# Attention scores of both heads as plain fp32 products in row halves, and all key tiles of the late queries turned by VectorE and DMAs

## The chip, the cores and the metric

One NeuronCore of a Trainium2 chip runs the whole kernel. The metric is device time in microseconds of one execution.

## The reference

A layer of post-norm attention followed by a routed feed-forward layer, all in fp32, on 8 sequences of 1024 tokens with 256 channels:

```python
latent_kv = x @ w_kv_down                 # rank 128
kv = latent_kv @ w_kv_up
k, v = (kv[..., :HD], kv[..., HD:])       # 16 heads of 64
q = (x @ w_q).reshape(Bx, Tx, N_HEAD, HEAD_SIZE)
att = jnp.einsum('bqhd,bkhd->bhqk', q, k) * scale
att = jnp.where(causal, att, -jnp.inf)
att = jax.nn.softmax(att, axis=-1)
y = jnp.einsum('bhqk,bkhd->bqhd', att, v)
x = layernorm(x + y.reshape(Bx, Tx, HD) @ w_out)
x = layernorm(x + experts(x))             # 8 experts, top tokens of each, gelu
```

The change is in the attention up to y; the output projection, the routing and the experts stay as they are.

## The kernel before, in words

`attention_stage` goes through 64 head pairs n (8 sequences, 8 pairs of heads each; "batch" is a sequence). Each engine has its own program, written out by hand, and semaphores tie them. A pair has 16 steps s, one for each query tile q = 0 to 7 of 128 queries and each head h. Query tile q has (q + 1) * 128 keys, since the mask is causal. For a step:

- TensorE computes the scores (`scores`, L443 and L444) into `s_ps`. Queries and keys are split in high and low fp32r parts. The tile `q_hl` of a head has the high part in the head's own 64 rows and the low part in the other 64; `k_hh` has the high keys in both halves, `k_lz` the low keys and zeros. So a first product gives high*high + low*high and a second high*low.
- VectorE adds the mask and takes the negated maximum (`maximum`, L734); ScalarE takes the exponential and its sum (`exp`, L623) into `prob`, one of four buffers; VectorE takes the reciprocal (`invert`, L739); GpSimd scales the tile (`norm`, L281).
- The probabilities are turned, so that keys lie in partitions. TensorE does it with an identity (`turn`, L453) for all tiles of q < 4 and for key tiles 0 to 3 of the late queries q >= 4; ScalarE and VectorE copy the result out of PSUM (`tri`, `prob_t`). Key tiles 4 to 7 of the late queries are turned in 32x32 squares by VectorE (`turn_squares`, L761) into `squares`; a DMA writes these to `s_d` in HBM (`write_squares`, L341) and four DMAs read them back, each to 32 partitions (`read_squares`, L349), into `late_t`.
- TensorE multiplies values and turned probabilities (`pv`, L476), 64 columns a head, so the two heads stand in the two column halves of the array: group 0 the early queries, group 1 the late ones. VectorE copies `o_ps` out (`copy_y`, L768), a DMA stores it.

Beside that, each pair needs projections of the pairs to come: queries (12 fp32r products of 512 columns, L519 to L521), keys (6, L532 to L534), values (8 fp32 products, L551). ScalarE takes the high part (`high`, L631), VectorE the low part (`low`, L747, L750), and ten DMAs of 256 KB (`place_queries`, `place_keys`) bring the parts to the rows where the scores want them. When a batch ends, the next x and its latents are split too. The order is set by tables, for instance

```python
SCORES_AT = [[4], [5], [6], [7], []] + [[s + 3] for s in range(5, 13)] + [[16], [17, 18], [19]]
INVERSES_AT = [[2], [3], [], [6], [7], []] + [[s + 2] for s in range(6, 16)]
Q_AT, K_AT, V_AT = (12, 15), (2, 5), (8, 10)
```

so the scores of a pair begin in the last steps of the one before, and the reading of `late_t` (`pv` of group 1, key tiles 4 to 7) stands in step 7 of the next pair. All DMAs here are issued by SP, one after the other (`turn` of the sync program).

Of the kernel before, what the change touches and what calls it, by code (L numbers as in the profile page):

```python
# [8 lines left out]
F32 = mybir.dt.float32  # L9
F32R = mybir.dt.float32r  # L10
# [29 lines left out]
class Bridge:  # L40
# [3 lines left out]
    def __init__(self, sb, sem, L):  # L44
# [3 lines left out]
        self.q_hl = [L.w1_hi[:, h * T:(h + 1) * T] for h in range(2)]  # L48
        self.k_hh = [L.w1_lo[:, h * T:(h + 1) * T] for h in range(2)]
# [4 lines left out]
        self.yt = [w[:].bitcast(F32).rearrange("p (m c) -> p m c", c=HALF) for w in (*self.q_hl, *self.k_hh)]  # L54
# [5 lines left out]
def attention_stage(nc, x_t, w_down, w_q, w_k, w_v, y_d, s_d, w_out, R):  # L60

    NPAIRS = B * NPAIR
    TRI = 2 * (4 + 3 + 2 + 1) * P

    Q = 32

    Q_AT, K_AT, V_AT = (12, 15), (2, 5), (8, 10)
    with ExitStack() as ctx:
# [4 lines left out]

# [3 lines left out]
        wd_hi = sb("wd_hi", [P, KC, RANK], F32R)  # L81
        wd_lo = sb("wd_lo", [P, KC, RANK], F32R)

        lat_hi = sb("b_lat_hi", [P, T], F32R)
        lat_lo = sb("b_lat_lo", [P, T], F32R)

        wqk = [sb(f"wqk{u}", [P, KC + 1, P]) for u in range(2)]
        wqk_hi = [sb(f"wqk_hi{u}", [P, KC + 1, P], F32R) for u in range(2)]
        wqk_lo = [sb(f"wqk_lo{u}", [P, KC + 1, P], F32R) for u in range(2)]
        wv = [sb(f"wv{u}", [P, P]) for u in range(2)]  # L90

        q_hl = [R.q_hl, [sb(f"q_hl1{h}", [P, T], F32R) for h in range(2)]]

        k_hh = [R.k_hh, [sb(f"k_hh1{h}", [P, T], F32R) for h in range(2)]]


        k_lz = [[sb(f"k_lz{u}{h}", [P, T], F32R) for h in range(2)] for u in range(2)]


        q_high, q_low, k_high, k_low = (sb(n, [P, T], F32R) for n in ("q_high", "q_low", "k_high", "k_low"))  # L100
        v = [sb(f"v{u}", [P, QT, P]) for u in range(2)]
        prob = [sb(f"prob{i}", [P, T]) for i in range(4)]

        wd = prob[3][:, 0:KC * RANK].rearrange("p (k r) -> p k r", r=RANK)

        tri = sb("tri", [P, TRI])
        prob_t = sb("prob_t1", [P, 2, 4, HALF])
        late_t = sb("late_t", [P, 4, 4, 8 * Q])  # L110

        squares = [sb(f"squares{i}", [P, (24 + 8 * i) * 4 * Q // 4]) for i in range(2)]
        neg_max = sb("neg_max", [P, 4])
        total = sb("total", [P, 4])
        inv = sb("inv", [P, 4])
# [7 lines left out]
        const_ready, x_in = sem("const_ready"), sem("b_x_in")  # L123


        x_then_q, wd_then_k = sem("x_then_q"), sem("wd_then_k")
# [5 lines left out]
        late_in = sem("late_in")  # L132
        squares_out = [sem(f"squares_out{i}") for i in range(2)]
        copied = [sem("copied_a"), sem("copied_d")]
# [5 lines left out]
        proj_done, high_done, low_done, v_copied, q_placed, k_placed = (  # L140
            sem(n) for n in ("proj_done", "high_done", "low_done", "v_copied", "q_placed", "k_placed"))
        block = ctx.enter_context(nc.Block())

        def step(s):

            return s // 8, 4 * (s // 8) + s % 8 // 2, s % 2

        def count(s):

            return min(4, step(s)[1] + 1)  # L150
# [11 lines left out]
        def square_part(w, h):  # L162

            return squares[(w - 1) % 2][:, 0:8 * w * Q].rearrange("p (j h k c) -> p j h k c", j=4, h=2, c=Q)[:, :, h, :, :]

        def late_row(h, k):

            at = k * 32 * Q + h * (k + 1) * Q + k * Q
            return bass.AP(tensor=late_t[:].tensor, offset=at, ap=[[128 * Q, P], [32 * Q + h * Q, 4 - k], [8 * Q, 4], [1, Q]])

        def turned_to(s):

            g, q, h = step(s)
            return tri_column(h, q) if g == 0 else prob_t[:, h, :, (q - 4) * P:(q - 3) * P]

        def score_at(s):

            return s_ps[s % 2], (s // 2 % 2 * HALF if s < 8 else 0)
# [1952 lines left out]
```

## Time and profile before

| | |
|---|---|
| median of 3 runs | 3088.05 us (3086.75 to 3089.26) |
| the profiled execution | 3095.27 us, its span 3093.4 us |
| TensorE, VectorE, ScalarE, GpSimd busy | 97%, 67%, 62%, 50% |
| mean granted TensorE clock | 0.989 |
| bytes moved by DMAs | 544.63 MB, mean 176 GB/s |
| HBM read, written | 213.16 MB, 159.47 MB |

Busy shares are of the span, in which the first 2040 us or so are the attention stage. A wait is idle time of an engine before an instruction, put down to what released it. A matmul's duration in a row includes its way through the array, so two that follow each other overlap: how much one costs is the distance of their starts. An fp32 product is two instructions on TensorE, an fp32r product one.

### The profile page before, as it was taken

The numbers are of one execution on the slowest core, as the hardware profiler recorded it, in microseconds if no ns is written. First come the engines' busy times: TensorE is split into PE (matmuls) and PEld (weight loads), VectorE is DVE, ScalarE is ACT, GpSimd is POOL, SyncE is SP. The second block draws the span as 40 slices with busy tenths as digits, with TensorE's granted clock in tenths as the row PEclk, the third lists the DMA queues.
The fourth block names the chain that finished last, engine by engine and source line by source line (L and its number), as shares of the span: only waits on it lengthen the run. The fifth ranks groups of instructions, "written<-read, shape, count | busy, mean of one in ns | idle before, by whom it ended". The sixth has DMA issues, their size and how long they took to land. (4 is left out here: it accounts for less than half of the span.)

```text
span 3093.4 us, 62741 instructions
## 1 busy us (share of the span) xinstructions
PE 2991.5 (97%) x19244; PEld 2394.3 (77%) x19244; DVE 2079.3 (67%) x5938; ACT 1910.0 (62%) x4173; POOL 1539.8 (50%) x1623
## 2 busy tenths in 40 slices
PE   8999999999999999999999999979989999999996
PEld 6776767776767776676767677679989999899996
DVE  6776777777767777676776777634968865545446
ACT  6676767777767777676767777635534444444443
POOL 4443444444444443444444344336767776666665
PEclk9999999999999999999999999989989999999998
DMA  7787877786777777777777787677734444434425
GB/s 182 202 205 186 205 207 190 202 212 188 201 205 189 196 202 192 197 198 208 186 203 209 192 208 203 167 242 267 242 112 122 115 103 105 106 78 91 110 50 163
DMA packets 397585, 544.63 MB, mean 176 GB/s; under 512 B 79528, under 2 KB 295976, under 8 KB 397248
## 3 DMA queue, kind: packets, MB, share of 16 engines
q1 hardware_dynamic: 355200, 490.05, 57.9%
q0 software_dynamic: 25152, 33.75, 6.6%
q10 hardware_dynamic: 16896, 16.78, 1.5%
q8 instruction: 157, 2.57, 0.3%
q14 instruction: 180, 1.47, 0.1%
HBM read 213.16 MB, written 159.47 MB: 120 GB/s over the span
## 5 line engine op out<-in xcount | busy, mean ns | idle before, releaser
L281 POOL TENSOR_SCALAR prob<-prob,inv 128x128 f32<-128x128 f32 (+7 forms) x1024 | 766.7, 752 | 1137.0 <-DVE inv L739 1136.6
L734 DVE CUSTOM_DVE_ANT_0 s_ps<-s_ps,mask 128x128 f32<-128x128 f32 (+7 forms) x1024 | 774.2, 756 | 445.1 <-PE s_ps L444 438.6
L623 ACT ACTIVATE prob<-s_ps,neg_max 128x128 f32<-128x128 f32 (+7 forms) x1024 | 760.3, 743 | 218.3 <-DVE neg_max L734 210.3
L453 PE MATMUL t_ps<-ident,prob 128*128 128x128 f32 x3328 | 527.3, 275 | 24.8 <-POOL prob L281 18.4
L453 PEld LDWEIGHTS t_ps<-ident,prob 128*128 128x128 f32 x3328 | 394.1, 141 | 75.9 <-POOL prob L281 23.4
L716 ACT ACTIVATE prob_t<-t_ps 128x512 f32<-128x512 f32 x512 | 305.8, 597 | 208.3 <-PE t_ps L453 208.2
L1791 PE MATMUL e_y<-w_hi,hid_hi 128*128 128x256 f32 (+1 forms) x1088 | 312.6, 287 | 0.0
L1793 PE MATMUL e_y<-w_hi,hid_lo 128*128 128x256 f32 (+1 forms) x1088 | 308.8, 284 | 0.0
L1792 PE MATMUL e_y<-w_lo,hid_hi 128*128 128x256 f32 (+1 forms) x1088 | 308.7, 284 | 0.0
L1652 POOL DMA_INDIRECT acc_d<-yg,idx_all x128 | 211.3, 1651 | 189.8 <-ACT yg L1865 160.9
L443 PE MATMUL s_ps<-w_lo,w_hi 128*128 128x512 f32 (+3 forms) x768 | 291.9, 382 | 7.4 <-ACT prob L623 7.4
L443 PE MATMUL s_ps<-k_hh,q_hl 128*128 128x512 f32 (+3 forms) x768 | 293.8, 385 | 4.6 <-ACT prob L623 4.5
L761 DVE STREAM_TRANSPOSE squares<-prob 128x128 f32<-128x128 f32 (+3 forms) x512 | 255.4, 499 | 54.2 <-DMA s_d<-squares 52.5
L1899 ACT ACTIVATE raw<-e_h,b1s 128x384 f32<-128x384 f32 (+3 forms) x336 | 193.8, 586 | 133.8 <-PE e_h L1774 128.3
L444 PE MATMUL s_ps<-k_lz,q_hl 128*128 128x512 f32 (+3 forms) x768 | 257.8, 348 | 0.0
L444 PE MATMUL s_ps<-k_lz,w_hi 128*128 128x512 f32 (+3 forms) x768 | 256.1, 346 | 0.0
L476 PE MATMUL o_ps<-prob_t,v 128*64 128x512 f32 x1024 | 237.1, 605 | 13.4 <-DMA late_t<-s_d 9.8
L1772 PE MATMUL e_h<-tok_hi,w_hi 128*128 128x384 f32 (+3 forms) x672 | 230.2, 343 | 1.7 <-DVE tok_lo L1937 1.2
L1773 PE MATMUL e_h<-tok_lo,w_hi 128*128 128x384 f32 (+3 forms) x672 | 230.1, 342 | 0.0
L1774 PE MATMUL e_h<-tok_hi,w_lo 128*128 128x384 f32 (+3 forms) x672 | 229.7, 342 | 0.0
L2033 DVE CAST hid_hi<-raw 128x384 fp32r<-128x384 f32 (+3 forms) x336 | 129.6, 386 | 121.9 <-ACT raw L1899 115.4
L1865 ACT ACTIVATE yg<-yb,gate_all 128x256 f32<-128x256 f32 x128 | 59.1, 502 | 239.6 <-DVE yb L2068 239.5
(261 smaller groups left out, 6732.0 us busy)
## 6 DMA issues: line engine op xcount, KB each, us to landing
k_hh<-k_high SPq DMA_DIRECT2D x128, 256.0 KB, 4.5
s_d<-squares SPq DMA_DIRECT2D x64, 512.0 KB, 3.0
y_d<-c_res SPq DMA_DIRECT2D x128, 256.0 KB, 4.0
late_t<-s_d SPq DMA_DIRECT2D x256, 128.0 KB, 3.3
k_lz<-k_low SPq DMA_DIRECT2D x126, 256.0 KB, 5.4
w_lo<-k_high SPq DMA_DIRECT2D x124, 256.0 KB, 4.5
c_yt<-y_d SPq DMA_DIRECT2D x60, 512.0 KB, 7.3
s_d<-squares SPq DMA_DIRECT2D x64, 384.0 KB, 2.6
```

The lines of the kernel that those rows point to most:

```text
L281: pool.tensor_scalar(pr, pr, inv[:, s % 4:s % 4 + 1], 1.0, ALU.mult, ALU.mult).then_inc(norm_done, 1)
L443: pe.matmul(out, q_hl[u][h][:, cols], k_hh[u][h][:, w], start=True, stop=False)
L444: mm = pe.matmul(out, q_hl[u][h][:, cols], k_lz[u][h][:, w], start=False, stop=True)
L453: mm = pe.transpose(t_ps[s % 2][:, to * P:(to + 1) * P], prob[s % 4][:, j * P:(j + 1) * P], ident[:])
L476: mm = pe.matmul(o_ps[64 * h:64 * h + 64, off:HALF], v[u][:, k, 64 * h:64 * h + 64], keys, start=(k == 0), stop=(k == 4 * g + 3), skip_gro ...
L623: act.activation(prob[s % 4][:, 0:(q + 1) * P], score_part(s), ACT.Exp, scale=-1.0, bias=neg_max[:, s % 4:s % 4 + 1], accum_out=total[:, s ...
L716: act.activation(turned_to(s), t_ps[s % 2][:, 0:count(s) * P].rearrange("p (j c) -> p j c", c=P), ACT.Copy).then_inc(copied[s % 2], 1)
L734: dve.tensor_tensor_reduce(part, part, mask[:, T - (q + 1) * P:T], 1.0, -MASKED, ALU.add, ALU.min, neg_max[:, s % 4:s % 4 + 1]).then_inc(m ...
L761: dve.transpose(square_part(w, h), prob[s % 4][:, HALF:HALF + w * P].rearrange("p (k j c) -> p j k c", j=4, c=Q)).then_inc(squared, 1)
L1791: pe.matmul(out, hid_hi[:, m, cols], w2_hi[u][:, w], start=(m == 0), stop=False)
L1792: pe.matmul(out, hid_hi[:, m, cols], w2_lo[u][:, w], start=False, stop=False)
L1793: mm = pe.matmul(out, hid_lo[:, m, cols], w2_hi[u][:, w], start=False, stop=(m == HC - 1))
```

## The change

Both heads' scores are fp32 products: head h uses rows 64h to 64h + 63 of the projected queries and keys where they are, one product for each head and 512 keys, in the two row halves of the array. The high and low parts of queries and keys, `low`, the zeros of `k_lz` and the ten placements a pair are gone. `turn` on TensorE and its copies are left for q < 4 alone; for q >= 4 all q + 1 key tiles go by `turn_squares`, `s_d` and `late_t`. `late_t` is double, `prob` has eight buffers in place of four, PSUM has three score units of two banks (one of them holds the turned early tiles), and `neg_max`, `total`, `inv` have eight columns. A reciprocal takes two heads at once. The output copies `copy_y` go from VectorE to ScalarE, the low parts of x and the latents of later batches from VectorE to GpSimd. The tables are replaced by eight slots a pair, one for each query tile; loops of SP are written out. The split weights and latents live in the space that `q_hl` and `k_hh` had.

The core of the diff (`-` before, `+` after):

```diff
-        s_ps = [pb(f"s_ps{i}", [P, T]) for i in range(2)]
-        t_ps = [pb(f"t_ps{i}", [P, HALF]) for i in range(2)]
+        s_ps = [pb(f"s_ps{i}", [P, T]) for i in range(3)]
...
+        def unit(n, role):
+            return s_ps[(role - n) % 3]
+
+        def score_part(n, s):
+            q, h = s // 2, s % 2
+            width = (q + 1) * P
+            if q < 4:
+                return unit(n, q % 2)[:, h * HALF:h * HALF + width]
+            return unit(n, (s - 8) % 3)[:, 0:width]
+
+        def turned_part(n, q, h):
+            return unit(n, 2)[:, h * HALF:h * HALF + (q + 1) * P]
...
-                    pe.matmul(out, q_hl[u][h][:, cols], k_hh[u][h][:, w], start=True, stop=False)
-                    mm = pe.matmul(out, q_hl[u][h][:, cols], k_lz[u][h][:, w], start=False, stop=True)
-                mm.then_inc(scores_done, 1)
...
+            def scores(n, q):
+                cols = slice(q * P, (q + 1) * P)
+                width = (q + 1) * P
+                for c in range(1 + q // 4):
+                    w = slice(c * HALF, min((c + 1) * HALF, width))
+                    for h in range(2):
+                        rows = slice(64 * h, 64 * h + 64)
+                        mm = pe.matmul(score_part(n, 2 * q + h)[:, w], q_of[n % 2][rows, cols], k_of[n % 2][rows, w],
+                                       start=True, stop=True)
+                        if c == q // 4:
+                            mm.then_inc(scores_done, 1)
...
+                elif q == 5:
+                    pe.wait_ge(copied, 4 * n + 4)
+                    pe.wait_ge(copied_last, n + 1)
+                    pe.wait_ge(exp_done, 16 * n + 9)
+                elif q > 5:
+                    pe.wait_ge(exp_done, 16 * n + 2 * q - 1)
...
+            def slot(n, q):
...
+                scores_free(n, q)
+                scores(n, q)
+                if q == 0:
+                    project_v(n, 0)
+                    if n >= 2:
+                        pv(n - 2, 1, [7])
+                if q == 1:
+                    project_v(n, 1)
+                    if n:
+                        pv(n - 1, 0, range(4))
+                    turn(n, 0)
+                if q == 2:
+                    if last_of_batch(n):
+                        project_l(n // NPAIR + 1, 0)
+                    turn(n, 1)
+                if q == 3:
+                    if last_of_batch(n):
+                        project_l(n // NPAIR + 1, 1)
+                    if after:
+                        project_q(n + 1, 0)
+                    turn(n, 2)
+                if q == 4:
+                    if after:
+                        project_k(n + 1, 0)
+                    turn(n, 3)
+                    if after:
+                        project_q(n + 1, 1)
+                if q == 5 and n:
+                    pv(n - 1, 1, [0, 1, 2])
+                if q == 6:
+                    if n:
+                        pv(n - 1, 1, [3, 4])
+                    if after:
+                        project_k(n + 1, 1)
+                if q == 7 and n:
+                    pv(n - 1, 1, [5, 6])
...
+            def turn_squares(n, q):
+                t = q + 1
+                for h in range(2):
+                    dve.wait_ge(norm_done, 16 * n + 2 * q + h + 1)
+                    if h == 0:
+                        dve.wait_ge(squares_out[q % 2], 16 * (2 * n + (q - 4) // 2))
+                    dve.transpose(square_all(q).rearrange("p (j h k c) -> p j h k c", j=4, h=2, c=Q)[:, :, h, :, :],
+                                  prob[(2 * q + h) % PB][:, 0:t * P].rearrange("p (k j c) -> p j k c", j=4, c=Q)
+                                  ).then_inc(squared, 1)
```

Slot q of a pair on VectorE has the two maxima of tile q; `turn_squares` of tiles 4 and 5 stand in slots 6 and 7, those of tiles 6 and 7 in slots 0 and 2 of the next pair. On ScalarE slot q has the two exponentials of tile q, on GpSimd the two norms.

Three places in the order. VectorE where one pair ends and the next begins; maxima are the rows with `s_ps,neg_max`, their width is the number of keys. Before:

```order
L734 ISA s_ps,neg_max<-s_ps,mask 128x1024 [waits scores_done]
L734 ISA neg_max 128x1
L739 RECIPROCAL inv<-total 128x1 [waits exp_done]
L761 STREAM_TRANSPOSE squares<-prob 128x4x96 [waits squares_out0,pv_done1,norm_done]
L734 ISA s_ps,neg_max<-s_ps,mask 128x128 [waits scores_done]
L734 ISA neg_max 128x1
L739 RECIPROCAL inv<-total 128x1 [waits exp_done]
L761 STREAM_TRANSPOSE squares<-prob 128x4x96 [waits squares_out0,pv_done1,norm_done]
```

Now:

```order
L631 ISA s_ps,neg_max<-s_ps,mask 128x1024 [waits scores_done]
L631 ISA neg_max 128x1
L637 RECIPROCAL inv<-total 128x2 [waits exp_done]
L645 STREAM_TRANSPOSE squares<-prob 128x4x192 [waits squares_out1,norm_done]
L645 STREAM_TRANSPOSE squares<-prob 128x4x192 [waits norm_done]
L631 ISA s_ps,neg_max<-s_ps,mask 128x128 [waits scores_done]
L631 ISA neg_max 128x1
L631 ISA s_ps,neg_max<-s_ps,mask 128x128 [waits scores_done]
L631 ISA neg_max 128x1
L645 STREAM_TRANSPOSE squares<-prob 128x4x224 [waits squares_out0,norm_done]
L645 STREAM_TRANSPOSE squares<-prob 128x4x224 [waits norm_done]
```

Turns of one head's squares, one between two maxima, have become two wide ones in a row, after both maxima of a tile. On TensorE, slots 5 to 7 of the new order (`tok` holds the queries and keys of every second pair):

```order
L323 MATMUL s_ps<-tok 128x256 x2
L368 MATMUL o_ps<-late_t,v 64x512 [waits y_copied,v_copied,late_in0]
L368 MATMUL o_ps<-late_t,v 64x512 x5
L323 MATMUL s_ps<-tok 128x512 [waits exp_done]
L323 MATMUL s_ps<-tok 128x512
L323 MATMUL s_ps<-tok 128x384 x2
L368 MATMUL o_ps<-late_t,v 64x512 x4
```

The products that read `late_t` now stand between the scores of tiles 5 and 6; the first of them waits for all 16 reads of the pair before. On SP, in each pair:

```order
L255 DMA s_d<-squares 128x2048 [waits squared]
L265 DMA late_t<-s_d 32x4x448 [waits squares_out0]
L265 DMA late_t<-s_d 32x4x448 x3
L250 DMA y_d<-c_res 128x512 [waits y_copied]
L265 DMA late_t<-s_d 32x4x512 [waits squares_out1]
L265 DMA late_t<-s_d 32x4x512 x3
L242 DMA wqk<-w_q 128x2x128 [waits proj_done]
```

The last write has 2048 columns where the largest had 1024, and the placements that stood behind the reads are gone.

## Rows read from the trace of the kernel before

**Rows 1.** the page, busy time, share of the span and instructions of each engine

```profile
PE 2991.5 (97%) x19244; PEld 2394.3 (77%) x19244; DVE 2079.3 (67%) x5938; ACT 1910.0 (62%) x4173; POOL 1539.8 (50%) x1623
```

**Rows 2.** the line of the masked maximum: count, min/median/max ns, first and last start

```profile
L734 DVE CUSTOM_DVE_ANT_0 s_ps<-s_ps,mask x1024: 266/775/1233, 23.9 to 2007.0; 128x128 f32<-128x128 f32 x22, 128x512 f32<-128x512 f32 x22, 128x896 f32<-128x896 f32 x22, 128x256 f32<-128x256 f32 x21
```

**Rows 3.** busy time by window: TensorE, weight load, VectorE, ScalarE, GpSimd, clock, DMA share, GB/s

```profile
600.00:900.00 300.00, 296.81 (x1778) 213.04 (x1779) 216.10 (x651) 214.86 (x508) 126.46 (x167) 1.00 0.76 201
```

**Rows 4.** timeline of TensorE in one pair: start us, us, engine, line, operation

```profile
641.40 3.65 PE L476 MATMUL o_ps<-prob_t,v 128*64 128x512 f32 x16
...
644.99 0.50 PE L443 MATMUL s_ps<-w_lo,w_hi 128*128 128x512 f32 x1
...
646.47 0.40 PE L443 MATMUL s_ps<-w_lo,w_hi 128*128 128x512 f32 x1
646.70 0.40 PE L444 MATMUL s_ps<-k_lz,w_hi 128*128 128x512 f32 x1
...
650.48 0.62 PE L453 MATMUL t_ps<-ident,prob 128*128 128x128 f32 x4
...
650.91 0.50 PE L443 MATMUL s_ps<-w_lo,w_hi 128*128 128x512 f32 x1
```

**Rows 5.** VectorE by form: busy us, mean ns, idle before

```profile
L734 DVE CUSTOM_DVE_ANT_0 s_ps<-s_ps,mask 128x1024 f32<-128x1024 f32 x128 | 156.0, 1219 | 65.1 <-PE s_ps L444 64.9 <-issue 0.2
...
L734 DVE CUSTOM_DVE_ANT_0 s_ps<-s_ps,mask 128x128 f32<-128x128 f32 x128 | 37.5, 294 | 47.7 <-PE s_ps L444 43.2
...
L761 DVE STREAM_TRANSPOSE squares<-prob 128x512 f32<-128x512 f32 x128 | 89.7, 701 | 6.9 <-DMA s_d<-squares 6.5 <-POOL prob L281 0.3
...
L761 DVE STREAM_TRANSPOSE squares<-prob 128x128 f32<-128x128 f32 x128 | 37.5, 293 | 0.0
```

**Rows 6.** timeline of VectorE, same pair

```profile
647.28 0.70 DVE L734 CUSTOM_DVE_ANT_0 s_ps<-s_ps,mask 128x512 f32<-128x512 f32 x1 [0.62 <-PE s_ps L444]
...
657.85 1.10 DVE L734 CUSTOM_DVE_ANT_0 s_ps<-s_ps,mask 128x896 f32<-128x896 f32 x1 [0.31 <-PE s_ps L444]
...
669.84 0.69 DVE L761 STREAM_TRANSPOSE squares<-prob 128x512 f32<-128x512 f32 x1
670.45 0.40 DVE L734 CUSTOM_DVE_ANT_0 s_ps<-s_ps,mask 128x256 f32<-128x256 f32 x1
```

**Rows 7.** DMA issues of the whole run: count, KB each, median us to landing

```profile
k_hh<-k_high SPq DMA_DIRECT2D x128, 256.0 KB, 4.5
...
s_d<-squares SPq DMA_DIRECT2D x64, 512.0 KB, 3.0
...
s_d<-squares SPq DMA_DIRECT2D x64, 384.0 KB, 2.6
...
late_t<-s_d SPq DMA_DIRECT2D x256, 128.0 KB, 3.3
```

**Rows 8.** timeline of ScalarE, same pair

```profile
659.04 1.01 ACT L623 ACTIVATE prob<-s_ps,neg_max 128x896 f32<-128x896 f32 x1 [0.31 <-DVE neg_max L734]
...
659.95 0.19 ACT L623 ACTIVATION_READ_ACCUMULATOR prob<-s_ps,neg_max 128x1 f32 x1
```

**Rows 9.** GpSimd by form

```profile
L281 POOL TENSOR_SCALAR prob<-prob,inv 128x1024 f32<-128x1024 f32 x128 | 143.2, 1118 | 109.1 <-DVE inv L739 109.1
...
L281 POOL TENSOR_SCALAR prob<-prob,inv 128x128 f32<-128x128 f32 x128 | 47.6, 372 | 150.6 <-DVE inv L739 150.5
```

**Rows 10.** timeline of the DMA queue, same pair

```profile
643.95 1.89 SPq L349 DMA_DIRECT2D late_t<-s_d  x4
```

**Rows 11.** timeline of TensorE around a stretch at half clock

```profile
918.38 0.90 PE L453 MATMUL t_ps<-ident,prob 128*128 128x128 f32 x4 [1.74 <-POOL prob L281]
...
919.50 0.63 PE L520 MATMUL j_ps<-b_xt_lo,wqk_hi 128*128 128x512 f32 x1
919.92 0.63 PE L521 MATMUL j_ps<-b_xt_hi,wqk_lo 128*128 128x512 f32 x1
```

**Rows 12.** busy time by window, the stretch at half clock

```profile
918.70:922.00 3.30, 3.30 (x12) 2.73 (x10) 2.29 (x8) 1.29 (x6) 0.59 (x2) 0.50 0.81 265
```

More of the change, by code:

```diff
@@ L195, in attention_stage @@
-        LATE_EXPS_AT = {0: [3]}
-        def over_pairs(eng, first, slots):
-            first()
-            for n in range(NPAIRS):
-                after = min(2, NPAIRS - 1 - n)
-                for g in range(2):
-                    slots(n, n % NPAIR, g, after)
-        X_SPLIT = [(NPAIR - 2, s) for s in (0, 2, 4, 6)]
-        L_AT = (11, 14)
-        W_SPLIT = 4
-        def x_piece(b, i):
-            if isinstance(b, int) and b == 0:
-                return i % 2, halves(i // 2)
-            return i // 2, halves(i % 2)
@@ new lines, in last_of_batch, with over_pairs, x_piece, x_pieces @@
+        def last_of_batch(n):
+            return n % NPAIR == NPAIR - 1 and n < NPAIRS - 1
+        def over_pairs(slot):
+            for n in range(NPAIRS):
+                for q in range(8):
+                    slot(n, q)
+        X_SPLIT = [(NPAIR - 2, 6), (NPAIR - 2, 7), (NPAIR - 1, 0), (NPAIR - 1, 1)]
+        def x_piece(i):
+            return i % 2, halves(i // 2)
+        def x_pieces(n, q):
+            at = (n % NPAIR, q)
+            return [X_SPLIT.index(at)] if at in X_SPLIT and n // NPAIR < B - 1 else []
@@ new lines, in turn @@
+            def turn(n, q):
+                if q:
+                    pe.wait_ge(copied, 4 * n + q)
+                elif n:
+                    pe.wait_ge(exp_done, 16 * n)
+                for h in range(2):
+                    pe.wait_ge(norm_done, 16 * n + 2 * q + h + 1)
+                    for j in range(q + 1):
+                        to = q - j if h else j
+                        mm = pe.transpose(turned_part(n, q, h)[:, to * P:(to + 1) * P],
+                                          prob[(2 * q + h) % PB][:, j * P:(j + 1) * P], ident[:])
+                    mm.then_inc(turned, 1)
@@ L616, in _ @@
+            over_pairs(slot)
+            pv(NPAIRS - 2, 1, [7])
+            pv(NPAIRS - 1, 0, range(4))
+            pv(NPAIRS - 1, 1, range(8))
         @block.scalar
@@ new lines, in exp, with keep @@
+                i = s % PB
+                act.activation(prob[i][:, 0:(q + 1) * P], score_part(n, s), ACT.Exp, scale=-1.0,
+                               bias=neg_max[:, i:i + 1], accum_out=total[:, i:i + 1]).then_inc(exp_done, 1)
+            def keep(n, i):
+                act.wait_ge(proj_done, proj(n, i))
+                to = (q_of, k_of)[i % 2][n % 2]
+                act.activation(to[:, halves(i // 2)], proj_bank(n, i), ACT.Copy,
+                               scale=1.0 if i % 2 else -SCALE).then_inc(high_done, 1)
```

793 lines of the change are left out of this document (326 added, 467 removed).

## The prediction

> **What bounds the kernel now.** I read the page first: TensorE is busy for 97% of the span, the next engine for 67% [rows 1]. Then the line of the masked maximum: 1024 of them, 16 a head pair, the first at 23.9 us and the last at 2007.0 us [rows 2], so a pair takes 1983/64 = 31.0 us and the change touches some 1984 us of the span. In a steady stretch, 600 to 900 us, TensorE is busy for 296.8 of 300 us at full clock, and VectorE, ScalarE and GpSimd for 216, 215 and 126 [rows 3]. The timeline of TensorE shows one product behind the other: the two passes of a 512-column score product start 0.23 us apart (646.47 and 646.70), four turns 0.43 us (650.48 to 650.91), the next product starts in the same moment [rows 4]. So a pair costs 31.0 us because TensorE has about that much to do.
>
> **TensorE's part.** Scores. A head's 36 key tiles of 128 columns took two passes of 0.23 us for 512 columns, 0.9 ns a column: 4.1 us, narrow ones a little more, 8.6 us for two heads, plus some 0.1 us at each of 16 entries after turns (a first product of 0.50 against 0.40 us in [rows 4]): 10.2. They become plain fp32 products with 64 rows, one head in each row half. No row shows row halves. The nearest shows fp32 in the two column halves: 16 instructions, two for each product, took 641.40 to 644.99 = 3.59 us for 4 key tiles of 512 columns and both heads [rows 4], so 0.43 us a pass for both heads together, 1.68 ns a column for a finished pair. I take that: 36 x 128 x 1.68 = 7.7 us and 8 entries of 0.1: 8.5. That is the lower end. The upper is the halves one after the other, 15.5 + 0.8. Turns: 32 of 52 go (four key tiles, two heads, four late query tiles), 32 x 0.108 = 3.5 us. Projections and values keep their products. TensorE: 31.0 - 1.7 - 3.5 = 25.8 us a pair. This alone would be a gain of 330 us, so the question is what is late next.
>
> The Trainium skill, TensorEngine Tiling, section Key Properties, says that a change of tiling mode drains TensorE. The run of 16 column-half products agrees weakly: 3.59 us against 8 x 0.43 = 3.44, so 0.15 for entry and exit. If a drain cost the pipeline's 0.35 us instead, the 16 changes of mode would add 4 us to TensorE and 0.75 to the loop below, giving some 3385.
>
> **The other engines.** VectorE loses the low halves (4 x 0.6), two output copies (1.2), the small copies and half the reciprocals, and turns 52 blocks in place of 20. A turn costs 0.293 us at 128 columns and 0.701 at 512 [rows 5], 0.136 for each further block: widths 640 to 1024 give 0.84, 0.97, 1.11, 1.25, less the 0.08 that consecutive operations overlap (669.84 to 670.45 is 0.61 for one of 0.69 [rows 6]). 7.7 us a pair against 3.4; all of VectorE about 20 us. ScalarE loses eight late copies and takes two output copies and four turned copies: 18 to 19. GpSimd 14. None of them fills 31 us, and none needs a price beyond these rows unless it stands in a chain.
>
> DMAs. Gone are ten placements of 256 KB a pair [rows 7]. Squares grow from 1.3 to 3.4 MB, written and read again: 7.7 MB a pair in place of 6.2. They were busy for 0.76 of the steady stretch [rows 3], so 0.95 of 31 us at the same efficiency, 29 us; the old placements had packets that were the slow ones, so likely less. Not the bound, but the round trip is longer.
>
> **The loop that I expect to set the time.** The new order on VectorE puts both turns of a query tile between one score group and the next, and SP carries them out and back. I follow what must follow what, from the scores of query tile 6 to the same scores one pair later (maximum 128 wide 0.294, 1024 wide 1.219 [rows 5], so 0.132 a block, 0.08 overlapped):
> - scores of tile 6: 896 x 1.68 + 0.1 = 1.6; to VectorE 0.35 (646.70 + 0.23 of columns to 647.28 in [rows 4, 6]);
> - maximum of tile 6 until its exponential starts 1.19 (657.85 to 659.04), that until its sum is read 1.12 [rows 6, 8]. The score unit of tile 7 is free only then;
> - scores of tile 7: 1.8 + 0.35; its two maxima 2.28; reciprocal and both turns of tile 5: 0.08 + 1.78;
> - next pair's maxima of tile 0: 0.43; both turns of tile 6: 2.06; maxima of tile 1: 0.65; reciprocals of tiles 7 and 0: 0.16, to GpSimd 0.25;
> - GpSimd: norms of tile 7 two x 1.12, of tile 0 two x 0.37 + 0.1 [rows 9]; the turn of tile 0 on TensorE 0.11; scores of tile 2: 0.74 + 0.35; maxima of tile 2: 0.96;
> - both turns of tile 7: 2.34 + 0.15; their 1 MB write. 512 KB land in 3.0 us, 384 KB in 2.6 [rows 7], 0.35 for 128 KB more: 4.5. The read, four DMAs of 256 KB issued over 2 us (the four of 128 KB took 1.89 [rows 10]); one of 128 KB lands 3.3 after its issue, and 1 MB more is on the way: 5.5;
> - the late product of values and tiles 0 to 2, 2.66 (three of 0.86, 0.1), stands ahead of the scores of tile 6.
>
> Sum: 1.95 + 1.19 + 1.12 + 2.15 + 2.28 + 1.86 + 0.43 + 2.06 + 0.65 + 0.41 + 2.24 + 0.84 + 0.11 + 1.09 + 0.96 + 2.49 + 4.5 + 5.5 + 2.66 = **34.5 us a pair**. TensorE idles about 9 of them, in four places: second values projection behind a ScalarE copy (slot 1), turn 0, turn 2, and the late product. Each batch edge adds the two latent projections and splits, some 3 us in 8 pairs: 34.9. That is 3.9 x 64 = +250 us. The profiled execution took 3095.3 us, 7 above the median: 3095 + 250 - 7 = 3338, and I say **3335**. Start and end change by a few us either way (no placements at the start; a longer trip at the end). The trip's price is my softest: at 0.85 and 1.15 of it the loop is 33.0 and 36.0, 3240 and 3430.
>
> **Rivals.**
> 1. The trip hides. If write and read take under 8 us in place of 10, a shorter loop decides: from the end of the turns of tile 7 (21.7) on, maximum of tile 6 of columns 0.62, reciprocal 0.33, norms of tile 2 1.27, turn 2 0.42, scores 4 1.17, projections and turn 3 3.1, scores 5 1.38, late product 2.66: 32.6, with edges 33.0: +128, 3216. For: landings there are seen beside 2.6 MB of placements that go.
> 2. The clock falls. It was granted at half from 918.7 to 922.0 us [rows 12], right after TensorE had waited 1.74 us for GpSimd with only narrow scores and turns around: the next 512-column products start 0.43 apart (919.50, 919.92), not 0.23 [rows 11]. The new order has waits of 1 to 3 us in each pair. Such a stretch of 3.3 us in each pair costs up to 1.7 us, most where TensorE has slack: at most +110, 3445. [...]
> 3. The row halves don't run together: the change doesn't do what it says. The loop's three score groups grow by 1.5, 1.7 and 0.6: 38.3, edges 38.7: +493, 3580. Against it: the column halves do.
> 4. **Faster**: TensorE still decides. Everything that I put in a chain would have to be ready earlier, so that less than 5.2 us of waits stand beside 25.8 us of work. Without waits 25.8 + 0.4 = 26.2: -307, 2780; with half of my waits 30.7, 3070. It decides from the point where the loop is below 31.0, 3.5 us under my sum; the trip at half its price and norms of tile 7 out of the way of tile 0 would do. For it speaks that each engine has a third of the time free; against it that the order is fixed and both engines take turns in it.
>
> **Numbers.** Forecast 0.51, rival 1 0.14, rival 2 0.14, rival 3 0.07, rival 4 0.14 (0.02 of it within the bound). The range takes the forecast with the trip's bounds, and rivals 1 and 2: 3180 to 3460, 0.79. A measurement of this kernel can tell 0.2%, 6 us, from no change. Faster 0.13 (rival 4 but for a sliver), same 0.02, slower 0.85.
>
> **What would show it.** Pair distance (last less first maximum, over 64) near 34.9. Scores: both heads' products start together, 0.43 us a 512-column pass; else rival 3. Waits of TensorE: late products for late_t, turns for prob by GpSimd, in sum 6 us a pair or more; if the DMA's share is nil, rival 1; if all are under 3, rival 4. s_d writes of 1 MB landing in 4 to 5 us. Granted clock under 0.95 in the attention stage: rival 2. If pair distance is right but waits stand elsewhere, the sum was luck.

## The result and the profile after

The changed kernel takes **3895.54 us** (median of 4 runs, 3890.03 to 3903.06), the kernel before beside it 3088.66 us (4 runs, 3086.75 to 3089.58). The ratio is 1.261, 95% interval 1.260 to 1.263: slower by 807 us. Forecast were 3335 us and a range up to 3460. The direction was right, the size was not. Two of the seven runs of the kernel before that stand beside e11 and e12 below were slow ones at a lower clock (3290 and 4837 us), and all ratios are of the fast runs.

The profiled execution took 3892.69 us, its span 3890.8, with a mean granted clock of 0.892 (before 0.989). TensorE is busy for 80% of the span, VectorE 51%, ScalarE 45%, GpSimd 40%: against [rows 1] no engine is busy throughout any more. The line of the masked maximum, with durations in ns and the first and last start in us:

```profile
engine op xcount: duration ns min/median/max, first and last start us, forms
L631 DVE CUSTOM_DVE_ANT_0 s_ps<-s_ps,mask x1024: 265/766/1267, 18.0 to 2795.6; 128x128 f32<-128x128 f32 x22, 128x512 f32<-128x512 f32 x22, 128x896 f32<-128x896 f32 x22, 128x256 f32<-128x256 f32 x21
```

(2795.6 - 18.0) / 64 = **43.4 us a pair**, against 31.0 before [rows 2] and 34.9 forecast. 12.4 us in 64 pairs are 794 of the 807 us, so nearly all of it is in the attention stage. The stretches of the steady part (busy us of each engine, then granted clock, share of the DMA engines, GB/s); the three short ones lie in one pair, and a share a little over 1 is to be read as full:

```profile
core 0: us, PE busy (x) PEld busy (x) DVE busy (x) ACT busy (x) POOL busy (x), PEclk, DMA share, GB/s
800.00:1200.00 400.00, 298.06 (x1395) 142.33 (x1391) 189.58 (x453) 183.28 (x455) 124.82 (x165) 0.86 0.66 181
938.00:943.00 5.00, 5.00 (x31) 3.27 (x27) 2.31 (x5) 3.13 (x7) 0.30 (x1) 1.00 0.97 224
943.00:948.00 5.00, 0.03 (x2) 0.00 (x0) 1.96 (x5) 1.93 (x4) 1.58 (x2) 0.71 1.06 245
948.00:950.60 2.60, 0.00 (x0) 0.00 (x0) 0.00 (x0) 0.00 (x0) 0.00 (x0) 0.50 0.78 130
```

TensorE's waits from 800 to 1200 us, which are 9.2 pairs (us in total, times, longest):

```profile
PE o_ps L368 <- DMA late_t<-s_d: 63.6, 9, 8.0
PE j_ps L429 <- ACT v L509: 20.6, 9, 2.3
PE s_ps L351 <- POOL prob L202: 16.2, 10, 1.8
```

Seven us a pair go to `late_t` alone. Around the longest wait the timeline of TensorE reads (start, us, and in brackets the idle time before):

```profile
936.00 1.02 PE L351 MATMUL s_ps<-ident,prob 128*128 128x128 f32 x6 [1.66 <-POOL prob L202]
936.95 1.35 PE L323 MATMUL s_ps<-tok 64*128 64x512 f32 x8
938.23 0.50 PE L414 MATMUL j_ps<-w_hi 128*128 128x512 f32 x1
...
941.47 1.56 PE L323 MATMUL s_ps<-tok 64*128 64x512 f32 x8
950.66 5.08 PE L368 MATMUL o_ps<-late_t,v 128*64 128x512 f32 x12 [7.63 <-DMA late_t<-s_d]
955.66 1.77 PE L323 MATMUL s_ps<-tok 64*128 64x512 f32 x8
```

and that of SP's queue:

```profile
934.49 0.34 SPq L255 DMA_DIRECT2D s_d<-squares  x1
934.94 2.91 SPq L265 DMA_DIRECT2D late_t<-s_d  x4
937.96 0.43 SPq L250 DMA_DIRECT2D y_d<-c_res  x1
939.71 1.73 SPq L265 DMA_DIRECT2D late_t<-s_d  x4
```

The turns of tile 7 are done at 934.5, and their write is issued. Its four reads are issued at 939.7, the product that needs them starts at 950.66. The trip from the last write to the late product is 16.2 us here, and the forecast had 10.0. The trace also has the landings: the last read of tile 6 at 944.4, the y store at 944.8, the four reads of tile 7 from 946.1 to 950.6. So of the 10.9 us after the write, the first 5.1 went by while the queue was still busy with what stood ahead. Then the late product of key tiles 0 to 2 takes 5.08 us, not 2.66: the clock fell to 0.50 during the wait. DMA issues and the queue's share from 800 to 1200 us (KB each, median us from issue to landing):

```profile
q1 hardware_dynamic: 34754, 72.05, 65.5%
...
s_d<-squares SPq DMA_DIRECT2D x10, 1024.0 KB, 5.1
late_t<-s_d SPq DMA_DIRECT2D x36, 256.0 KB, 7.5
late_t<-s_d SPq DMA_DIRECT2D x40, 224.0 KB, 6.9
```

The scores did what the change says: in the timeline above the eight instructions of tile 4 take 1.28 us to the start of the next product (936.95 to 938.23), and one pair earlier those of tile 6 take 1.70 (912.11 to 913.81):

```profile
912.11 1.77 PE L323 MATMUL s_ps<-k,q 64*128 64x512 f32 x8
913.81 1.94 PE L368 MATMUL o_ps<-late_t,v 128*64 128x512 f32 x8
```

The forecast had 1.2 and 1.6. The two row halves run side by side. By the forecast's 1.68 ns a column, 0.2 us of each group, up to the start of the next product, are not columns, where the sum had 0.1; and the scores of tile 5 start 0.32 us after a product (941.15, 941.47) whose like lie 0.23 apart. The reading that gave 3385 us had 0.35 at each change of mode, more than either.

### The profile page after: what moved, and what is told of

The parts are those of the page before. It is cut to its first block and busy times, and to the rows that moved or that the text cites. A ratio compares the mean times of both kernels' runs of the same rounds, so it can differ in the third digit from the quotient of the medians.

```text
span 3890.8 us, 53342 instructions
## 1 busy us (share of the span) xinstructions
PE 3104.0 (80%) x17196; PEld 1979.4 (51%) x17196; DVE 1968.5 (51%) x4808; ACT 1766.1 (45%) x3981; POOL 1570.1 (40%) x1661
## 5 line engine op out<-in xcount | busy, mean ns | idle before, releaser
L368 PE MATMUL o_ps<-late_t,v 128*64 128x512 f32 (+3 forms) x2048 | 557.9, 679 | 469.8 <-DMA late_t<-s_d 469.8
L368 PEld LDWEIGHTS o_ps<-late_t,v 128*64 128x64 f32 x2048 | 153.2, 167 | 801.2 <-DMA late_t<-s_d 495.4
L645 DVE STREAM_TRANSPOSE squares<-prob 128x640 f32<-128x640 f32 (+3 forms) x512 | 500.9, 1016 | 2.0 <-DMA s_d<-squares 2.0
L323 PE MATMUL s_ps<-k,q 64*128 64x512 f32 (+3 forms) x1536 | 322.7, 525 | 3.4 <-ACT prob L498 3.4
L323 PE MATMUL s_ps<-tok 64*128 64x512 f32 (+3 forms) x1536 | 321.4, 523 | 3.6 <-ACT prob L498 2.6
L351 PE MATMUL s_ps<-ident,prob 128*128 128x128 f32 x1280 | 212.5, 287 | 106.1 <-POOL prob L202 105.5
L429 PE MATMUL j_ps<-wv,b_lat 128*128 128x128 f32 x1024 | 165.0, 309 | 144.5 <-ACT v L509 144.1
L351 PEld LDWEIGHTS s_ps<-ident,prob 128*128 128x128 f32 x1280 | 141.1, 142 | 209.0 <-issue 142.9
L368 PE MATMUL o_ps<-tri,v 128*64 128x512 f32 (+3 forms) x1024 | 240.5, 633 | 3.1 <-ACT c_res L523 3.1
L429 PEld LDWEIGHTS j_ps<-wv,b_lat 128*128 128x128 f32 x1024 | 137.3, 208 | 178.3 <-ACT v L509 170.2
```

The costliest lines, as they stand in the source:

```text
L323: mm = pe.matmul(score_part(n, 2 * q + h)[:, w], q_of[n % 2][rows, cols], k_of[n % 2][rows, w], start=True, stop=True)
L351: mm = pe.transpose(turned_part(n, q, h)[:, to * P:(to + 1) * P], prob[(2 * q + h) % PB][:, j * P:(j + 1) * P], ident[:])
L368: mm = pe.matmul(o_ps[64 * h:64 * h + 64, off:HALF], v[n % 2][:, k, 64 * h:64 * h + 64], keys, start=(k == 0), stop=(k == 4 * g + 3), skip ...
L645: dve.transpose(square_all(q).rearrange("p (j h k c) -> p j h k c", j=4, h=2, c=Q)[:, :, h, :, :], prob[(2 * q + h) % PB][:, 0:t * P].rear ...
```

## The experiments

Each kernel is the changed one with the edit shown. Its time stands beside runs of the kernel before on the same chip (medians 3088 to 3094 us). "A pair" is the last less the first maximum of the profiled run, over 64, as above.

| run | edit | us | ratio, interval | us a pair | clock, 800 to 1200 us |
|---|---|---|---|---|---|
| before | | 3088 | | 31.0 | |
| changed | | 3895.5 | 1.261 [1.260, 1.263] | 43.4 | 0.86 |
| e1 | no reads | 3297.6 | 1.068 [1.065, 1.071] | 34.4 | 0.96 |
| e2 | reads from two queues | 3834.0 | 1.241 [1.238, 1.245] | 42.5 | 0.86 |
| e3 | filler in the wait | 3772.2 | 1.221 [1.218, 1.225] | 41.5 | 0.96 |
| e4 | late product later | 3580.1 | 1.159 [1.154, 1.165] | 38.4 | 0.92 |
| e5 | spread reads, VectorE pays | 3809.3 | 1.234 [1.230, 1.237] | 42.1 | 0.87 |
| e6 | e5 and e4 | 3730.8 | 1.208 [1.202, 1.215] | 40.8 | 0.88 |
| e7 | spread reads, TensorE pays | 3775.8 | 1.221 [1.209, 1.232] | 41.8 | 0.94 |
| e8 | e7 and e4 | 3750.5 | 1.213 [1.209, 1.216] | 41.2 | 0.92 |
| e9 | spread reads, keys dealt by ScalarE | 3607.9 | 1.167 [1.143, 1.190] | 39.3 | 0.91 |
| e10 | e9 and e4 | 3352.7 | 1.084 [1.079, 1.089] | 35.0 | 0.96 |
| e11 | e10 in a new order | **3015.9** | **0.976 [0.974, 0.978]** | 29.8 | 1.00 |
| e12 | the new order, reads as changed | 3240.1 | 1.048 [1.046, 1.051] | 33.2 | 0.97 |

### Is it the trip? e1, e2

```diff
-                read_squares(n, 4)
+                if n < 2:
+                    read_squares(n, 4)
```

The same for tiles 5 to 7; the waits for `late_t` are on the constant 256. From the third pair on the late product takes what the first two pairs left, so the late queries are not computed. The writes stay.

> The change with the read back of the squares left out from the third pair on (the late products then use old rows of late_t, so the late queries of the output are not the reference's). Writes stay. Theory A (the loop through the trip of the squares sets the pair, and its price was 16 us where 10 were put down): the loop without the trip decides, 32.6 us in steady pairs by the sum of the prediction, 33 with batch edges, and the granted clock of the attention stage rises from 0.86 to over 0.95, since the wait of 7 us goes: some 3220 us, 43.4 to 33 us a pair. Theory B (the clock at half is what costs, the waits are its consequence): the pair falls less, to 38 or more, the clock stays under 0.9. Theory C (TensorE alone would decide without the trip): under 28 us a pair, 2900 us.

Measured: 3297.6 us, 34.4 us a pair. TensorE's waits, for 11.6 pairs:

```profile
PE j_ps L433 <- ACT v L513: 27.5, 12, 2.3
PE s_ps L355 <- POOL prob L202: 20.1, 17, 1.9
```

The time fell with the reads as theory A has it, but 78 us less far than its 3220. So the reads carry 598 of the 807 us; what is left without them, the writes and the order of the engines, 1.4 us a pair above what rival 1 summed, carries the other 209. Of that order one sees two waits: 2.4 us a pair for ScalarE's copy of the values and 1.7 for GpSimd's norms.

```diff
-                for j in range(4):
+                for j in range(2):
...
+                for j in range(2, 4):
+                    act.dma_start(late_t[n % 2][Q * j:Q * j + Q, q - 4, :, 0:2 * t * Q],
```

> The change with two of the four reads of each tile (partitions 64 to 127) issued from ScalarE's queue, so that both halves of the partitions are written at the same time; same bytes, same waits of TensorE. Theory A1 (reads are slow because each read, and so all engines at one time, writes 32 partitions: 228 KB a us in the trace of the change): reads go to 350 to 390 KB a us, the trip from the write of tile 7 to the late product falls from 16 to 11 or 12 us, the pair from 43.4 to 38 or 39, some 3590 us. Theory A2 (the reads are limited by HBM or by the bytes of all DMAs together): no change beyond 1 us a pair, packets of 2048 bytes still take 135 ns at twice the number in flight; ScalarE's issues cost up to 1 us a pair.

Measured: 3834.0, 42.5 us a pair, and a trip of 15.9 us in the pair at 917 us. 256 KB landed in 6.8 us from SP and 8.1 from ScalarE (7.5 before the edit). Theory A1, which had 3590 us, failed: in that pair the reads of tile 7 landed one after the other all the same, those of SP at 928.4 and 929.8, those of ScalarE at 930.7 and 932.5. The issuing is not what makes the reads slow. Whether their partitions are, this edit can't tell.

### How much is the clock? e3

```diff
+                    if after:
+                        pe.wait_ge(high_done, 4 * n + 7)
+                        for _ in range(FILL):
+                            pe.matmul(j_ps[:, 0:256], wd_hi[:, 0, :], wd_hi[:].rearrange("p k r -> p (k r)"),
+                                      start=True, stop=True)
```

56 products a pair, with no use for their result, stand ahead of the late product.

> The change with 56 extra fp32r products of 256 columns (about 6.2 us at full clock) on TensorE between the scores of tile 5 and the late product, into the projection bank, so that TensorE works while it waits for the reads. Nothing else moves. Theory A (half clock after the long wait adds 1.5 to 2.4 us to the late product and about 1 us to the scores and values behind it, all on the loop): late product of tiles 0 to 2 falls from 4.3 to 5.1 us to 2.7, the clock of the stage rises from 0.86 to over 0.95, the pair falls by 2 to 3 us to about 41, some 3740 us. Theory B (the clock's loss lies in slack): clock up, pair unchanged within 0.5 us.

Measured: 3772.2, 41.5 us a pair, **1.9 less**, though work was added. The clock in the window went from 0.86 to 0.96 and the 512-column late products from a mean of 852 ns to

```profile
L369 PE MATMUL o_ps<-late_t,v 128*64 128x512 f32 x180 | 42.6, 602 | 3.9 <-DMA late_t<-s_d 3.9
```

That is just under the 2 to 3 us of theory A. So the fall of the clock behind the long wait costs about 1.9 us a pair, and it costs them on the loop, since the late product is the first thing that the wait holds up.

### How much room does the trip need? e4

```diff
-                if q == 5 and n:
-                    pv(n - 1, 1, [0, 1, 2])
...
-                        pv(n - 1, 1, [3, 4])
+                        pv(n - 1, 1, [0, 1, 2])
```

The rest of the late product follows one tile later too.

> The change with the late products of a pair moved one slot back: tiles 0 to 2 behind the scores of tile 6 (not 5), 3 and 4 in slot 7, 5 to 7 in slot 0. Same work, same bytes. Theory A (the loop goes trip, late product, scores 6, maximum and exponential 6, scores 7): scores 6, its maximum and exponential now run beside the trip, so 1.6 + 0.35 + 2.3 = 4.3 us leave the loop less what the new order adds before copy_y: the pair falls by 3 to 4.5 us to 39 to 40.5, some 3680 us; the wait for late_t falls from 7.5 us to 3 to 4. Theory B (DMA throughput, not the loop, sets the pair): unchanged within 0.5 us, the wait only moves.

Measured: 3580.1, 38.4 us a pair, 5.0 less, more than the 3 to 4.5 expected. The wait for `late_t` is down to 2.5 us a pair (10.4 pairs), and the next ones have come forward:

```profile
PE o_ps L368 <- DMA late_t<-s_d: 25.5, 10, 3.5
PE s_ps L323 <- ACT prob L496: 25.1, 11, 2.3
PE s_ps L351 <- POOL prob L202: 24.3, 26, 2.3
```

### Why are the reads slow? e5 to e10

The four reads of a tile write 32 neighbouring partitions each. In the steady part the queue moved 72.05 MB with 16 engines busy for 65.5% of 400 us: 275 KB per us of full use. In two stretches of the pair shown above in which nearly nothing but these reads ran, the last column shows 226 and 209 GB/s:

```profile
939.70:941.20 1.50, 1.50 (x10) 1.18 (x8) 1.10 (x3) 1.50 (x5) 0.00 (x0) 1.00 0.99 226
945.00:948.00 3.00, 0.00 (x0) 0.00 (x0) 0.18 (x2) 1.20 (x4) 1.04 (x2) 0.51 1.06 209
```

The placements of the kernel before wrote 64 neighbours, and a stretch of them alone (its 648 to 652 us) has 221 GB/s at a share of 0.98. In e5 key 4c + j of a tile, in place of 32j + c, goes to group j, so that a read writes partitions j, j + 4, ..., j + 124.

```diff
-                    sp.dma_start(late_t[n % 2][Q * j:Q * j + Q, q - 4, :, 0:2 * t * Q],
+                    sp.dma_start(late_t[n % 2][j:P:4, q - 4, :, 0:2 * t * Q],
...
-                                  prob[(2 * q + h) % PB][:, 0:t * P].rearrange("p (k j c) -> p j k c", j=4, c=Q)
+                                  prob[(2 * q + h) % PB][:, 0:t * P].rearrange("p (k c j) -> p j k c", j=4, c=Q)
```

> The changed kernel with the keys of a tile dealt out otherwise: key 4c + j, in place of 32j + c, goes into group j, so each of the four reads of a tile writes the 32 partitions j, j + 4, ..., j + 124 of late_t and not 32 neighbours. Same bytes, same packets, same order; VectorE's block turns read their input at a step of four numbers. Theory A (a read is slow because it reaches only part of the way into SBUF: neighbours share it, spread partitions don't; the placements of the kernel before, on 64 neighbours, went at the same 219 GB/s): the reads' rate rises from about 228 to 350 KB/us or more, the trip from the last write to the late product falls from 16.2 to 11 to 12 us, the wait for late_t in a pair from about 7 us to 2 to 3, the pair from 43.4 to 38 to 39.5 us: 3700 to 3760 us. Theory B (the read side or the size of the pieces sets the rate): the rate stays under 250, the time within 1% of 3895, or above it if the turns grow by the step.

> The spread reads together with the late product one tile later, as in the run with the late product later (3580, 38.4 us a pair, there still 2.5 us a pair of waits for late_t). Theory A: the wait for late_t goes to nothing and what is left is the loop without the trip, as in the run without reads (34.4 us a pair), and contention of what still moves: 35 to 37 us a pair, 3330 to 3480. Theory B: no gain over 3580.

Measured: e5 3809.3, e6 3730.8. The reads did become fast:

```profile
late_t<-s_d SPq DMA_DIRECT2D x36, 256.0 KB, 5.0
...
late_t<-s_d SPq DMA_DIRECT2D x36, 224.0 KB, 5.1
```

against 7.5 and 6.9. But VectorE reads at a step of four numbers now, and a block turn of 1024 columns went from 1219 ns to

```profile
L645 DVE STREAM_TRANSPOSE squares<-prob 128x1024 f32<-128x1024 f32 x18 | 35.3, 2008 | 0.0
```

Eight turns a pair are longer by 5.3 us together, on a loop in which VectorE's turns stand. So e5 won 86 us where 135 to 195 were expected, and e6, expected at 3330 to 3480, was slower than e4. The two edits changed two prices at once. In e7 and e8 VectorE turns neighbours again, and TensorE takes the keys at the step, as the moving operand of the late scores (with a mask in that order).

```diff
+                    keys_in = lambda k: k if q < 4 else k.rearrange("p (k c j) -> p k j c", j=4, c=Q)
...
-                        mm = pe.matmul(score_part(n, 2 * q + h)[:, w], q_of[n % 2][rows, cols], k_of[n % 2][rows, w],
+                        mm = pe.matmul(score_part(n, 2 * q + h)[:, w], q_of[n % 2][rows, cols], keys_in(k_of[n % 2][rows, w]),
```

> The spread reads without their price on VectorE: in the run with spread reads the reads landed in 5.0 us in place of 7.5, but a block turn of 1024 columns took 2.01 us in place of 1.22, and the time fell only to 3809. Here VectorE's turns read 32 neighbouring columns again; in their place TensorE takes the keys of the late tiles at a step of four columns as the moving operand of the scores (with a mask in that order), and the reads still write partitions j, j + 4, ... Theory A (the reads are slow by the partitions that they reach, and the trip is on the loop): the 256 KB reads land in about 5 us, the block turns are back at 1.2 us, the wait for late_t falls from 7 us a pair to about 3, the pair from 43.4 to 38 to 40 us: 3550 to 3720. Theory B (the reads' rate matters little, because what is late next takes the place): 3750 or more. If TensorE is slower with a step of four columns, the scores of tiles 4 to 7 show it (1.35 us of 8 instructions for tile 5 now).

> The same with the late product one tile later. The trip is then off the loop by theory A, and the loop without it is what the run without reads showed, 34.4 us a pair and 3298: expected 34.5 to 36.5, 3300 to 3450. Theory B (the stall behind the reads was only half of it and contention keeps the rest): 37.5 or more, within 3% of the 3580 of the late product alone.

Measured: 3775.8 and 3750.5, where 3550 to 3720 and 3300 to 3450 were expected; by the letter of the expectations theory B held. But the price had moved to TensorE. Its forms from 800 to 1200 us in e7:

```profile
L330 PE MATMUL s_ps<-tok 64*128 64x512 f32 x120 | 55.7, 1027 | 0.0
...
L375 PE MATMUL o_ps<-late_t,v 128*64 128x512 f32 x180 | 47.0, 655 | 9.3 <-DMA late_t<-s_d 9.3
```

This form was 644 ns in the changed kernel. In e9 and e10 ScalarE deals the keys out once a pair, where it copies them out of PSUM, and one more copy keeps the first 512 in their old order for the early tiles.

```diff
+                    if i == 1:
+                        act.activation(k_e, proj_bank(n, i), ACT.Copy)
+                    act.activation(k_of[n % 2][:, halves(i // 2)].rearrange("p (k j c) -> p k j c", j=4, c=Q),
+                                   proj_bank(n, i).rearrange("p (k c j) -> p k j c", j=4, c=Q), ACT.Copy
```

> The spread reads with the new key order made by ScalarE where it copies the keys out of PSUM, once per pair, so that neither VectorE's turns nor TensorE's scores read at a step (on VectorE the step took a turn of 1024 columns from 1.22 to 2.01 us; on TensorE it took a 512-column score product from 0.64 to 1.03 us, which gave back most of what the reads won). One more copy of 512 columns on ScalarE keeps the first keys in their old order for the early tiles. Theory A (the rate of the reads is a cause, and the two runs before hid it behind a slower engine): 256 KB reads land in 5 us, score products and turns as in the changed kernel, waits for late_t 2 to 3 us a pair in place of 7, the pair 38.5 to 40 us in place of 43.4: 3560 to 3650. Theory B (what is late next takes all of it): 3750 or more. A step that makes ScalarE's copies longer shows in their mean (0.48 us now).

> The same, with the late product one tile later. Theory A: no wait for late_t is left, late product at most 3.5 us; the loop is that of the run without reads, 34.4 us a pair, plus what transfers still in the way cost: 34.5 to 36.5 us a pair, 3300 to 3460. Theory B (the order of the other engines binds at 38 whatever the reads do): 3550 or more.

Measured: **3607.9 and 3352.7**, both as expected (e9 in two runs that lie apart, 3591.1 and 3624.8). The step costs ScalarE nothing (the copy in the old order is the first line):

```profile
L513 ACT ACTIVATE both_all<-j_ps 128x512 f32<-128x512 f32 x10 | 6.0, 597 | 13.0 <-PE j_ps L424 13.0
L514 ACT ACTIVATE k<-j_ps 128x512 f32<-128x512 f32 x10 | 5.9, 590 | 0.0
```

The DMAs of e9, for the rows of the changed kernel above:

```profile
q1 hardware_dynamic: 38419, 79.44, 58.9%
...
late_t<-s_d SPq DMA_DIRECT2D x40, 256.0 KB, 4.9
...
late_t<-s_d SPq DMA_DIRECT2D x40, 224.0 KB, 5.1
```

79.44 MB at 58.9%: 337 KB per us of full use in place of 275. The same bytes in the same packets, other partitions. TensorE's waits of e9, for 10.2 pairs:

```profile
PE o_ps L376 <- DMA late_t<-s_d: 32.4, 10, 4.3
PE j_ps L437 <- ACT v L523: 25.2, 11, 2.3
```

The wait for `late_t` went from 7 us a pair to 3.2. The Trainium skill, SBUF — State Buffer, section "Door 1: The DMA port swizzle", says that a transfer's rate depends on how many of 16 ports its partitions reach, and that partitions 0 to 31 or 0 to 63 reach eight, some 218 GB/s at most. The runs agree: 226 and 209 GB/s in the two stretches of reads on 32 neighbours, 221 in that of placements on 64. They do not show ports as such. The same page's section "Can I just issue two DMAs to hit both halves?" says that two transfers do not reach both halves together, and that only one transfer spanning all 128 partitions reaches all 16 ports. e2 agrees with the first. As to the second, 32 partitions at a step of four, which lie over all 128 but are no more than 32, were faster than 32 neighbours: it was the spread of the partitions that did it, not their number.

With the late product later (e10) the wait for `late_t` is gone but for 0.5 us in 400, and a pair takes 35.0 us, nearly as good as without any reads (34.4). What is left, for 11.4 pairs, is the order:

```profile
PE s_ps L331 <- ACT prob L504: 27.4, 12, 2.3
PE s_ps L359 <- POOL prob L209: 23.9, 25, 2.3
```

### The order itself: e11, e12

e11 is e10 with the steps of each engine in another order, nothing added and nothing left out. TensorE's order for a pair (S scores, V, Q, K, L projections, T turns, P early product, p, r, s the late one in three parts):

```diff
-S0 V0 p S1 V1 P0 T0 S2 L0 T1 S3 L1 Q0 T2 S4 K0 T3 Q1 S5 S6 r K1 S7 s
+S0 V0 p S1 V1 S2 P0 L0 T0 S3 T1 L1 Q0 T2 S4 K0 T3 Q1 S5 K1 S6 r S7 s
```

GpSimd takes the next pair's norms of tile 0 ahead of those of tile 7; ScalarE copies the first values at once; VectorE turns tiles 4 and 5 ahead of the maxima of tiles 6 and 7, and the last pair's tile 7 between the two maxima of tile 2.

> The last kernel (keys dealt out, late product one tile later) with the steps of each engine in another order, nothing added or left out. What stood on its loop by its waits: TensorE waits 2.3 us a pair for the exponentials of tile 5 ahead of the scores of tile 6, 2.1 for the norms ahead of the turns, 0.6 for the copy of the values. So GpSimd takes the norms of the next pair's tile 0 ahead of those of tile 7; TensorE turns tiles 0 and 1 one tile later and projects the second keys ahead of the scores of tile 6; ScalarE copies the values at once; VectorE turns tiles 4 and 5 ahead of the maxima of tiles 6 and 7, and tile 6 and 7 ahead of the next pair's early maxima. Theory A (with the trip off the loop, the loop is the order of the engines, and TensorE's work of 25.8 us a pair is the floor): a pair of 29.5 to 32 us in place of 35.0: 3000 to 3170, about the kernel before (31.0 us a pair). Theory C (contention, or a clock that falls with the wait, holds the pair near 35 whatever the order): 3300 or more.

> The same new order and the late product one tile later, but with the reads on 32 neighbouring partitions, as in the changed kernel. If the two causes (the rate of the reads, the order) are apart, the trip of some 16 us binds again: a wait for late_t of 3 to 5 us a pair comes back, the pair at 33 to 35.5 us, 3220 to 3400. If the order alone were the cause, it comes within 1% of the run above.

Measured for e11: **3015.85 us** (4 runs, 3015.16 to 3019.12), 2.4% below the kernel before. Its maxima, stretches, the largest wait of TensorE and the DMAs:

```profile
L594 DVE DVE_READ_ACCUMULATOR2_ANT neg_max<- x1024: 83/142/144, 18.2 to 1927.9; 128x1 f32 x171
```

```profile
800.00:1200.00 400.00, 373.75 (x2021) 194.69 (x2023) 279.51 (x651) 270.27 (x675) 182.96 (x238) 1.00 0.78 264
1600.00:2000.00 400.00, 354.05 (x2006) 200.29 (x2003) 256.81 (x583) 241.77 (x576) 169.81 (x215) 0.96 0.77 263
```

```profile
PE s_ps L346 <- ACT prob L495: 17.7, 13, 1.4
```

```profile
q1 hardware_dynamic: 51450, 105.14, 77.5%
...
late_t<-s_d SPq DMA_DIRECT2D x56, 256.0 KB, 4.9
```

29.8 us a pair, and in the window TensorE is busy for 374 of 400 us at full clock: it is nearly the bound again, with less to do than in [rows 3]; from 1600 to 2000 us it is 354, at a clock of 0.96. 105.14 MB at 77.5% are 339 KB per us. e12, the same order with the reads on neighbours, came to 3240.1, as expected if the two causes are apart: the wait for `late_t` is back at 2.6 us a pair (12 pairs; 3 to 5 were expected), and the queue is at 86%:

```profile
PE o_ps L383 <- DMA late_t<-s_d: 31.3, 10, 3.9
PE s_ps L338 <- ACT prob L487: 15.9, 13, 1.6
```

```profile
q1 hardware_dynamic: 44994, 92.29, 85.9%
...
late_t<-s_d SPq DMA_DIRECT2D x48, 256.0 KB, 7.2
```

Order and reads are two causes, and both have to go. The four kernels with the late product later make a square: the new order brings 340 us with reads on neighbours (e4 to e12) and 337 with spread ones (e10 to e11), the spread reads 227 in the old order (e4 to e10) and 224 in the new one (e12 to e11). So the two gains add.

## Why the prediction was wrong

**TensorE's part** was right. The row halves run together, tile 6 in 1.70 us for 1.6. 25.8 us a pair was a little low: e11 shows 374 and 354 busy us in two windows of 13.4 pairs, 27.9 and 26.4.

**The other engines** were right: the turn of 1024 columns took 1.22 us (1.25 forecast).

**The DMAs, 29 us and "Not the bound",** were right as a mean and wrong as an argument. 0.66 x 43.4 is 28.6 us a pair, nearly to the point. But the mean says nothing of how long the last transfer of a pair waits: between 938 and 948 us the queue was full (shares 0.97 and 1.06), and from 943 on TensorE stood behind it. The step also took comfort in the placements that go. It missed that the reads write neighbouring partitions as those did, and that 2.1 MB more of them come in their stead.

**The trip in the loop, 4.5 us for the write and 5.5 for the read,** is the step that failed. Measured 5.2 and 10.9. The read was priced from the growth of the *writes* with size [rows 7] and from a queue with the last 1 MB alone in it. In truth tile 6's reads, a y store and then tile 7's stand in one queue, and stretches of such reads moved 209 and 226 GB/s. With spread reads the trip falls from 16.2 to 13.0 us (e9: write issued 934.15, late product 947.15), so 3.2 of the missing 6.2 us are the partitions. The other 3.0 are put down to what stands ahead in the queue, which no run took away by itself.

**The late product, 2.66,** took 4.27 and 5.08 us in two pairs, after waits of 7.15 and 7.63 us, and 2.80 in a pair of e9, after a wait of 1.33. The mean of one of its 512-column instructions was 852 ns in place of 602 (e3). This is rival 2, named right (clock 0.86 in the attention stage, under 0.95) but priced "most where TensorE has slack", and put at nothing in the sum. The clock falls because TensorE waits, and so it is low just when the awaited data land, at the head of the loop's next piece: e3 gives 1.9 us a pair.

**The rest of the loop** came out as summed. From the scores of tile 6 (912.11) to the same scores a pair later (955.66) are 43.55 us: 22.4 to the last write for 21.8, 16.2 for the trip for 10.0, 5.0 for the late product for 2.66. The differences of 0.6, 6.2 and 2.3 are the 9.1 us by which this pair is longer than the sum of 34.5. Of the four places where TensorE was to idle, three show: the values, the turn of tile 2 and the late product. Ahead of the turn of tile 0 it came late by itself, 0.3 us after GpSimd's norms, so that piece of the chain ran over TensorE's values and early product and had nearly the forecast length by luck.

**Rival 1**, the trip hidden, is what e1 and e10 show, with its sum 1.4 to 2.0 us low: 34.4 and 35.0 us for 33.0. **Rival 3** fell. **Rival 4** was no way for this kernel, but its condition, "norms of tile 7 out of the way of tile 0" and a shorter trip, is near to what e11 does, where the trip still takes its time (256 KB land in 4.9 us) but stands off the loop: 29.8 us a pair, in its range. The third of each engine's time that it called free was to be had.

The range failed for the same reason as the sum: it varied the trip by 15% where it was off by 62%, with a term from rows of writes, and it took the clock as a rival beside the trip, when the one brings the other.

## What to carry to other kernels

Price a round trip to HBM by the queue as it will stand when the last transfer is issued, and a read by the partitions that it writes: here 32 neighbours took 7.5 us and 32 spread ones 4.9. Dealing the data out was dear in VectorE's turns and TensorE's products and free in a copy that ScalarE made anyway. Where a change makes a long wait of TensorE on the loop, as the 7 us here, add that the work behind it may start at half clock; such a wait costs more than its length. And when a change takes work from the bound and the time rises, look at the chain before giving up the change: with fast reads, the trip off the loop and each step where its inputs are ready, this one went from 1.26 to 0.98 of the kernel before.

## What the runs showed of the hardware that was not expected

- A VectorE block turn that reads SBUF at a step of four fp32 numbers took 2008 ns for 1024 columns, against 1219 without the step (e5).
- TensorE's fp32 product of 512 columns with the moving operand at a step of four took 1017 to 1032 ns in the mean, against 635 to 644 in the changed kernel (e7, e8).
- ScalarE reading PSUM at the same step and writing SBUF in a row took 590 ns, no more than the plain copy's 597 (e9).
- Reads from HBM of the same bytes and packets landed in 4.9 to 5.0 in place of 7.5 us when their 32 partitions were spread over all 128 (e5, e9), and issuing half of them from another engine's queue left their landing about as it was, 6.8 and 8.1 us (e2).
